# Causal attention in a decoder layer: who adds up the diagonal tiles, inverts the denominators and writes the upper output half

## What is computed

```python
x = _layernorm(x + _L0_attn_ref(x, Wqkv, Wout, bout))          # causal, 16 heads of 32
x = _layernorm(x + _L0_xattn_ref(x, ctx, ctx, mask, ...))      # cross attention
x = _layernorm(x + _L0_ffn_ref(x, w1, b1, w2, b2, ...))        # 8 experts, top 2

# _L0_attn_ref
qkv = x @ Wqkv.T
dots = where(causal_mask, -inf, einsum('bhid,bhjd->bhij', q, k) * dh**-0.5)
out = einsum('bhij,bhjd->bhid', softmax(dots), v)
return out @ Wout.T + bout
```

## Time and profile before

| | |
|---|---|
| median of 3 runs | 2791.89 us (2785.82 to 2792.28) |
| profiled execution | 2788.14 us, its span 2786.3 us |
| TensorE busy | 2563.3 us (92%) |
| VectorE busy | 1913.3 us (69%) |
| ScalarE busy | 1102.4 us (40%) |
| GpSimd busy | 782.0 us (28%) |
| self-attention within the span | about 290 to 1520 us |

### The profile page before, as it was taken

How to read it: one execution, slowest core, us unless ns; L and a number is a source line. 1 busy time by engine, 2 the same in 40 slices (tenths; PEclk the granted TensorE clock), 3 DMA queues, 4 the chain that set the end, 5 groups by cost and what they waited for, 6 DMA issues and landing times. The chain is left out here.

```text
span 2786.3 us, 44691 instructions
## 1 busy us (share of the span) xinstructions
PE 2563.3 (92%) x15124; PEld 1064.3 (38%) x15124; DVE 1913.3 (69%) x3125; ACT 1102.4 (40%) x2002; POOL 782.0 (28%) x276
## 2 busy tenths in 40 slices
PE   8999699998999899999998679999999999999998
PEld 3444223232232233332322335454544544454543
DVE  5442787877778677778882557776867676767764
ACT  4231155555555455555555223231323323232320
POOL 0000254553636344445455211111201011111100
PEclk9999799999999999999999889999999999999999
DMA  7953500302020302012001210101010101001000
GB/s 245 306 193 140 122 9 6 73 6 70 9 69 9 69 6 55 23 34 74 5 12 56 86 43 1 58 1 59 1 43 16 43 16 43 16 1 58 1 16 16
DMA packets 115902, 146.74 MB, mean 53 GB/s; under 512 B 9086, under 2 KB 87678, under 8 KB 114653
## 3 DMA queue, kind: packets, MB, share of 16 engines
q1 hardware_dynamic: 115677, 143.77, 16.9%
HBM read 91.57 MB, written 51.91 MB: 51 GB/s over the span
## 5 line engine op out<-in xcount | busy, mean ns | idle before, releaser
L715 ACT ACTIVATE probs<-st_ps 128x512 f32<-128x512 f32 (+3 forms) x1280 | 628.2, 533 | 590.5 <-PE st_ps L821 294.6
L746 DVE TENSOR_REDUCE seg_max<-s_ps 128x1 f32<-128x512 f32 (+3 forms) x1280 | 699.8, 599 | 230.3 <-PE s_ps L804 136.9
L804 PE MATMUL s_ps<-k_pair,q_pair 96*128 96x512 f16 (+3 forms) x1280 | 438.7, 364 | 70.0 <-DVE seg_max L746 56.4
L821 PE MATMUL st_ps<-q_pair,k_pair 98*128 98x512 f16 (+3 forms) x1280 | 434.6, 360 | 26.6 <-issue 19.5
L623 POOL TENSOR_TENSOR total<-total,probs 128x2048 f32<-128x2048 f32 x88 | 398.2, 4525 | 62.1 <-ACT probs L715 59.6
L841 PE MATMUL o_ps<-probs,v_sb 128*32 128x512 f32 (+3 forms) x2560 | 321.4, 572 | 0.7 <-issue 0.7
L1381 PE MATMUL fps<-x2T,w_p_hi 128*128 128x512 f16 x1024 | 317.2, 379 | 0.0
L1381 PE MATMUL fps<-w_p_hi,hT 128*128 128x512 f16 x1024 | 306.0, 381 | 0.0
L821 PEld LDWEIGHTS st_ps<-q_pair,k_pair 98*128 98x128 f16 x1280 | 117.5, 98 | 374.4 <-ACT probs L715 287.4
L804 PEld LDWEIGHTS s_ps<-k_pair,q_pair 96*128 96x128 f16 x1280 | 125.6, 99 | 276.9 <-DVE seg_max L746 191.3
L1343 DVE SCALAR_TENSOR_TENSOR x<-fps,gates_un,x 128x512 f32<-128x512 f32 x256 | 184.0, 746 | 36.0 <-PE fps L1381 33.4
(11 more groups left out here) (162 smaller groups left out, 3553.7 us busy)
## 6 DMA issues: line engine op xcount, KB each, us to landing
k_pair<-k_parts SPq DMA_DIRECT2D x96, 128.0 KB, 5.0
q_pair<-q_parts SPq DMA_DIRECT2D x96, 128.0 KB, 5.6
x_raw<-xT_in SPq DMA_DIRECT2D x8, 1024.0 KB, 6.5
q_parts<-qk_out SPq DMA_DIRECT2D x32, 256.0 KB, 3.6
k_parts<-qk_out SPq DMA_DIRECT2D x32, 256.0 KB, 4.0
piece_raw<-w_in SPq DMA_DIRECT2D x8, 1024.0 KB, 8.7
v_rows<-v_out SPq DMA_DIRECT2D x32, 256.0 KB, 2.1
w_parts<-piece_cut SPq DMA_DIRECT2D x8, 1024.0 KB, 5.6
```

Of the source, the lines that this page charges most:

```text
L715: nc.scalar.activation(probs[:, k % NP, h, off:], st_ps[:, p % (2 * NVU) % RING, off:], ACT.Exp, scale=SCALE).then_inc(exp_done.sem, 1)
L746: nc.vector.reduce_max(seg_max[:, h, j, s:s + 1], s_ps[:, slot, 0:width], AX.X).then_inc(s_read.sem, 1)
L804: last = nc.tensor.matmul(s_ps[:, slot, 0:width], q_pair[a][0:NR, h, q0:q0 + P], k_pair[a][0:NR, h, s * CH:s * CH + width], start=True, st ...
L821: last = nc.tensor.matmul(st_ps[:, slot, off:], k_pair[a][:, h, kt * P:(kt + 1) * P], q_pair[a][:, h, c * CH + off:(c + 1) * CH], start=Tr ...
```

## The change

- GpSimd also adds up all diagonal tiles, each over the columns that count. In chunk 0 the first addition starts at column 128, and a copy brings the rest. TensorE makes no sums for diagonal tiles any more; the matmuls over `total` become a step of their own, `totals`, with lag 8, in every chunk. `o_ready` goes (the values of the last tile count in `pv_done`), `den_ready` comes.
- ScalarE takes `den` with lag 9. One row of each head's 32 equal rows is moved to `inv_small`, 128 partitions x 16 columns (lag 10), VectorE inverts that (lag 16), SyncE stores it to a DRAM tensor `inv_rows` (17), and four broadcasting loads spread it over `inv` (21). GpSimd multiplies with lag 25.
- ScalarE instead of VectorE writes the upper half (lag 27), GpSimd the rest (28), the store has lag 29, and the tail of the plan is 30 steps instead of 21.
- `o_raw` and `den` get two buffers.

```diff
@@ -422,17 +422,20 @@
     NKU, NVU, NAUX = len(KU), len(VU), len(AUX)
-    POOLED = [[n for n, (k, kt) in enumerate(KU) if k == c and kt < c * TT and kt % 3 != 2]
+    POOLED = [[n for n, (k, kt) in enumerate(KU) if k == c and (kt >= c * TT or kt % 3 != 2)]
               for c in range(CPB)]
     ADDS = [n for tiles in POOLED for n in tiles[1:]]
     NP = 5
     RING = 3
-    PIECES = 4
     VALUES, SUMS = 4, 6
-    TAKEN = VALUES + 1, SUMS + 1
-    RECIPS = [SUMS + 3 + 2 * n for n in range(PIECES)]
-    SCALED = RECIPS[-1] + 1
+    TOTALS = 8
+    TAKEN = VALUES + 1, TOTALS + 1
+    DEN_MOVED = TAKEN[1] + 1
+    INVERTED = DEN_MOVED + 6
+    INV_STORED = INVERTED + 1
+    INV_LOADED = INV_STORED + 4
+    SCALED = INV_LOADED + 4
     STORED = SCALED + 4
     TAIL = STORED + 1
     READY = 6
...
@@ -447,8 +450,7 @@
         steps = [0.06 + 0.6 * (CH - off(c, kt)) / CH for c, kt, _ in VU]
         busy = [0.0] * NVU
         for t in LAST_TILE:
-            for lag in RECIPS:
-                busy[(t * HG + HG - 1 + lag) % NVU] += 0.85
+            busy[(t * HG + HG - 1 + INVERTED) % NVU] += 0.2
         cost = []
         for what, c, unit in AUX:
             if what == "rows":
...
@@ -549,8 +551,10 @@
-        o_raw = sb("o_raw", [P, CH], F32)
-        den = sb("den", [P, CH], F32)
+        o_raw = sb("o_raw", [P, 2, CH], F32)
+        den = sb("den", [P, 2, CH], F32)
+        inv_small = sb("inv_small", [P, 2, CH // DH], F32)
+        inv = sb("inv", [P, 2, CH], F32)
...
@@ -613,20 +619,26 @@
                     c, n = KU[k % NKU][0], adds_upto(k) - 1
                     starts = k % NKU == POOLED[c][1]
                     pool.wait_ge(exp_done.sem, exp_done.at(i, HG * k + HG - 1))
+                    off = max(KU[k % NKU][1] - c * TT, 0) * P
                     if starts:
-                        pool.wait_ge(pv_done.sem, pv_done.at(i, k // NKU * NKU + LAST_TILE[c - 1]))
+                        pool.wait_ge(den_ready.sem, den_ready.at(i, k // NKU * CPB + c - 1))
                         other = probs[:, (k // NKU * NKU + POOLED[c][0]) % NP]
                     else:
                         pool.wait_ge(added.sem, added.at(i, n - 1))
                         other = total[:]
-                    nc.gpsimd.tensor_tensor(total[:], other, probs[:, k % NP], ALU.add).then_inc(added.sem, 1)
+                    last = nc.gpsimd.tensor_tensor(total[:, :, off:], other[:, :, off:], probs[:, k % NP, :, off:],
+                                                   ALU.add)
+                    if starts and off:
+                        last = nc.gpsimd.tensor_copy(total[:, :, 0:off], other[:, :, 0:off])
+                    last.then_inc(added.sem, 1)
                 c = chunk_at(s, SCALED, first, end)
                 if c is not None:
-                    pool.wait_ge(recips.sem, recips.at(i, c * PIECES + PIECES - 1))
+                    pool.wait_ge(inv_loaded, 16 * HG * (2 * CPB * i + c + 1))
                     pool.wait_ge(split_done.sem, split_done.at(i, c - 1))
-                    nc.gpsimd.tensor_tensor(o_sb[:], o_raw[:], den[:], ALU.mult).then_inc(scaled.sem, 1)
+                    nc.gpsimd.tensor_tensor(o_sb[:], o_raw[:, c % 2], inv[:, c % 2],
+                                            ALU.mult).then_inc(scaled.sem, 1)
                 c = chunk_at(s, SCALED + 3, first, end)
                 if c is not None:
                     pool.wait_ge(o_hi_done.sem, o_hi_done.at(i, c))
...
@@ -674,6 +686,21 @@
                     sp.wait_ge(pv_done.sem, pv_done.at(i, k))
                     for c in range(CPB):
                         load(2 * i + k // NKU + 2, k // NKU % 2, c)
+                c = chunk_at(s, DEN_MOVED, first, end)
+                if c is not None:
+                    sp.wait_ge(den_taken.sem, den_taken.at(i, c))
+                    sp.dma_start(inv_small[:, c % 2], den[0:P:DH, c % 2]).then_inc(den_moved, 16)
+                c = chunk_at(s, INV_STORED, first, end)
+                if c is not None:
+                    sp.wait_ge(recips.sem, recips.at(i, c))
+                    sp.dma_start(inv_rows[c % 2].rearrange("h (a b) -> (h a) b", b=CH // DH),
+                                 inv_small[:, c % 2]).then_inc(inv_stored, 16)
+                c = chunk_at(s, INV_LOADED, first, end)
+                if c is not None:
+                    sp.wait_ge(inv_stored, 16 * (2 * CPB * i + c + 1))
+                    for h in range(HG):
+                        sp.dma_start(inv[h * DH:(h + 1) * DH, c % 2], inv_rows[c % 2, h].partition_broadcast(
+                            DH)).then_inc(inv_loaded, 16)
                 c = chunk_at(s, STORED, first, end)
                 if c is not None:
                     sp.wait_ge(split_done.sem, split_done.at(i, c))
...
@@ -716,19 +744,24 @@
                                          scale=SCALE).then_inc(exp_done.sem, 1)
                 c = chunk_at(s, TAKEN[0], first, end)
                 if c is not None:
-                    act.wait_ge(o_ready.sem, o_ready.at(i, c))
-                    act.wait_ge(scaled.sem, scaled.at(i, c - 1))
-                    nc.scalar.activation(o_raw[:], o_ps[:], ACT.Copy).then_inc(o_taken.sem, 1)
+                    act.wait_ge(pv_done.sem, pv_done.at(i, c // CPB * NKU + LAST_TILE[c % CPB]))
+                    act.wait_ge(scaled.sem, scaled.at(i, c - 2))
+                    nc.scalar.activation(o_raw[:, c % 2], o_ps[:], ACT.Copy).then_inc(o_taken.sem, 1)
                 c = chunk_at(s, TAKEN[1], first, end)
                 if c is not None:
-                    act.wait_ge(pv_done.sem, pv_done.at(i, c // CPB * NKU + LAST_TILE[c % CPB]))
-                    nc.scalar.activation(den[:], den_ps[:], ACT.Copy, scale=1.0 / XS).then_inc(den_taken.sem, 1)
+                    act.wait_ge(den_ready.sem, den_ready.at(i, c))
+                    nc.scalar.activation(den[:, c % 2], den_ps[:], ACT.Copy, scale=1.0 / XS).then_inc(den_taken.sem, 1)
+                c = chunk_at(s, SCALED + 2, first, end)
+                if c is not None:
+                    act.wait_ge(scaled.sem, scaled.at(i, c))
+                    act.wait_ge(o_stored[c % 2], stored_at(CPB * i + c // 2))
+                    nc.scalar.activation(o_out[:, c % 2, 0], o_sb[:], ACT.Copy).then_inc(o_hi_done.sem, 1)
             laps(act, step)
         @block.vector
         def _(dve):
-            for count in (s_read, max_ready, steps, recips, o_hi_done):
+            for count in (s_read, max_ready, steps, recips):
                 count.lead(dve)
             def aux(i, n):
...
@@ -758,18 +791,10 @@
             def step(i, s, first, end):
                 for n in aux_at(s, first, end):
                     aux(i, n)
-                for n, lag in enumerate(RECIPS):
-                    c = chunk_at(s, lag, first, end)
-                    if c is not None:
-                        if n == 0:
-                            dve.wait_ge(den_taken.sem, den_taken.at(i, c))
-                        piece = den[:, n * CH // PIECES:(n + 1) * CH // PIECES]
-                        nc.vector.reciprocal(piece, piece).then_inc(recips.sem, 1)
-                c = chunk_at(s, SCALED + 2, first, end)
+                c = chunk_at(s, INVERTED, first, end)
                 if c is not None:
-                    dve.wait_ge(scaled.sem, scaled.at(i, c))
-                    dve.wait_ge(o_stored[c % 2], stored_at(CPB * i + c // 2))
-                    nc.vector.tensor_copy(o_out[:, c % 2, 0], o_sb[:]).then_inc(o_hi_done.sem, 1)
+                    dve.wait_ge(den_moved, 16 * (2 * CPB * i + c + 1))
+                    nc.vector.reciprocal(inv_small[:, c % 2], inv_small[:, c % 2]).then_inc(recips.sem, 1)
             for n in range(AHEAD):
                 aux(0, n)
...
@@ -842,27 +867,28 @@
                                             start=(kt == 0), stop=final)
                 if k % NKU in POOLED[c]:
                     last.then_inc(pv_done.sem, 1)
-                elif final:
-                    last.then_inc(o_ready.sem, 1)
             def sums(i, k):
                 c, kt = KU[k % NKU]
-                off, pooled = max(kt - c * TT, 0) * P, POOLED[c]
-                final = k % NKU == LAST_TILE[c]
-                if k % NKU in pooled:
+                if k % NKU in POOLED[c]:
                     return
-                opens = all(n in pooled for n, (x, _) in enumerate(KU) if x == c and n < k % NKU)
+                opens = all(n in POOLED[c] for n, (x, _) in enumerate(KU) if x == c and n < k % NKU)
                 if opens:
                     pe.wait_ge(den_taken.sem, den_taken.at(i, k // NKU * CPB + c - 1))
                 for h, out in enumerate(heads):
-                    last = nc.tensor.matmul(den_ps[out, off:], ones[:], probs[:, k % NP, h, off:], start=opens,
-                                            stop=final and not pooled)
-                if final and pooled:
-                    pe.wait_ge(added.sem, added.at(i, adds_upto(k) - 1))
```

(16 more changed lines are left out.)

14 lines of the change are left out of this document (9 added, 5 removed).

## The result

The changed kernel takes 2861.27 us, median of four runs (2857.15 to 2866.8); the kernel before, beside it, 2790.48 us (2785.82 to 2792.28). The ratio is 1.0258, with an interval of 1.0235 to 1.0280. So the change makes the kernel 2.6% slower. The forecast was slower too, and 2861 lies inside the range, but the size is far off: 20 us were forecast, 71 came.

The account below looks back on a forecast made before the run. TensorE was taken as the bound. From 2788.1 us, 61 gained in eight groups, 75 lost to denominators waiting behind loads and 6.7 at the stage's end gave 2808.8, taken as 2808; range 2735 to 2870.

Parts of the forecast that it names:

- VectorE's wait behind the loads: At the end of 6 of 8 groups, chunk 3's denominator transfer queues behind SyncE's loads: VectorE stands 18 us, TensorE 15.5.
- 3.7 for the clock: After TensorE's stall behind the loads: further loss at lower clock, 3.7 us for each of six sets of loads.
- 3.5 absorbed: After the stall behind loads, slow steps absorb chunk 3's ScalarE wait: 3.5 us taken off each, 21 in all.
- Rival 1: SyncE's queue: small transfer held only behind the loads' issue, not their data; TensorE stands 9 us; total 2769; chance 0.16.
- ScalarE's two long waits: Upper half's wait for GpSimd's multiplication: 4.5 us for chunk 3, 6 for chunk 0; TensorE stands 2.9 and 4.8.
- Rival 2: Behind `max_parts`, VectorE's subtraction waits out a second, back-to-back GpSimd addition: 4.52 us once a group; total 2844; chance 0.17.
- Rival 3: Queues absorb it: ScalarE's waits vanish in TensorE's lead, a group takes 131 us; total 2741; chance 0.17.
- rival 4: Whole kernel: gain and loss cancel, the work merely changes its owner; total 2788; chance 0.12.
- the last diagonal addition ends before TensorE asks for it: GpSimd's queue, followed at the tile pace: its diagonal sums are ready before TensorE needs them, two tiles later.
- a stretch at half clock: TensorE behind a stall: part of the following time runs at 1.2 instead of 2.4 GHz, costing about 1.7 us each.
- The chain behind it: End of the stage, from `den` through small transfers and reciprocal to the last store: issued 6.7 us later, uncovered.
- a gain of 12.0 us a group: VectorE's casts removed: 6.9 us of TensorE's idle time and 5.1 us at half clock taken as gone.

Follow-up runs that it names:

- g4: Changed kernel with ScalarE's upper half, GpSimd's subtraction and the store six steps later, loads left in place: 2817.56 us, 1.0102 against the kernel before.
- e1: Changed kernel with SyncE's loads moved away from the groups' ends, 78 and 126 steps after: 2755.8 us, 0.9880 against the kernel before.
- f1: e1 with ScalarE's upper half, GpSimd's subtraction and the store six steps later: 2708.77 us, 0.9717 against the kernel before.
- g1: f1 with ScalarE instead of VectorE scaling the row maxima into `max_parts`: 2663.29 us, 0.9549 against the kernel before.
- g2: g1 with the last chunk's diagonal sums on TensorE in the last group only: 2651.87 us, 0.9500 against the kernel before.
- e2: Control: kernel before the change with the loads moved to the same two places as in e1: 2782.36 us, 0.9976 against the kernel before.
- f4: Kernel before with only GpSimd's diagonal additions and two buffers for denominators and raw outputs: 2900.25 us, 1.0404 against the kernel before.
- f2: e1 with the sums over diagonal tiles back on TensorE: 2761.77 us, 0.9908 against the kernel before.
- e4: Changed kernel with the `max_parts` scaling written as an operation with two SBUF inputs: 2863.92 us, 1.0266 against the kernel before.
- f3: e1 with the upper half written by VectorE instead of ScalarE, at the same step: 2750.43 us, 0.9864 against the kernel before.

## Why the prediction was right or wrong

**Where the miss lies.** In the profiled executions 20.7 us were forecast and 69.0 measured. Of the 48.3 us between them 21.8 lie in the six groups between the cuts, 20.2 in the two groups outside them with the end of the stage, 6.2 in the second half.

**Right: the mechanism, and the price of the wait partly by luck.** VectorE's wait behind the loads was forecast at 18 us, TensorE's at 15.5: 17.19 and 16.54. One set of loads was to cost 15.5 + 3.7 for the clock - 3.5 absorbed, 15.7 us: 15.2. But the last two terms are both wrong and cancel. In a group with loads (611.43 to 772.06) TensorE still waits 8.2 us for ScalarE, against 7.9 in the one without, so nothing is absorbed, and g4 says the same. Its busy time there is 129.7 us against 129.2, so the clock adds 0.5 and not 3.7. What the six groups of before already held of it (19.6) is also right: 901.3 us are 6 x 147.0 and 19.3. And e1 shows by experiment what the trace could only suggest. Rival 1 (a shorter wait) fell: the transfer was held by both the issue order and its own issue of 6.24 us.

**Right: what moved.** GpSimd's 114.7 us a group are 115.15. TensorE waits 61.7 us for ScalarE, which is 7.7 a group, as forecast, and again two errors cancel. ScalarE's two long waits were forecast at 4.5 and 6 us, of which the score banks were to keep 2.8 from TensorE; they are shorter, and TensorE stands 3.71 and 4.20 us behind them, so that only 0.5 is kept. The four waits of ScalarE in the group without loads are 3.82, 4.61, 0.82 and 0.43 us. These are the rows of the first two:

```profile
1448.07 0.63 ACT L758 ACTIVATE o_out<-o_sb 128x512 f16<-128x512 f32 x1 [3.82 <-POOL o_sb L640]
1467.27 0.63 ACT L758 ACTIVATE o_out<-o_sb 128x512 f16<-128x512 f32 x1 [4.61 <-POOL o_sb L640]
```

TensorE waits 28.0 us for `max_parts`, 3.5 a group against 3.8 forecast. Rival 2 fell for the changed kernel: the subtraction behind takes 176 ns on average over 30, with GpSimd busy for 80% of a group. Its mechanism is real all the same and was a matter of 0.1 us: f1's rows show it at 4.42 us once a group, which is what the rival had said. Rival 3 (the queues absorb it) fell by the 61.7 us above, rival 4 (nothing) by the result.

**Wrong: the ordinary group, 143.5 us and not 139.4.** That is 4.1 us in each of the eight, 33 in all; the 21.8 and the 20.2 us above both hold their share of it. Two terms of the sum failed. The first is the sentence "the last diagonal addition ends before TensorE asks for it". It doesn't:

```profile
1373.72 1.93 PE L890 MATMUL den_ps<-total,ones 128*32 128x512 f32 x8 [2.38 <-POOL total L630]
```

That happens once a group, 17.4 us in the eight groups, 2.2 a group. I had followed the queue at a pace of 2.75 us for a diagonal tile, but its additions take 4.5 and 3.4 us for the first two, and by my reading the queue was not empty when they came. The prediction named this very wait as what would prove it wrong. The second is the clock. TensorE's busy time came out at 129.15 us where the terms gave 127.1 (138.1 - 11.0, less the 5.1 us for the casts, plus 3.4 and 1.7). I had charged a stretch at half clock that loses 1.7 us for each of three stalls. Before, that is right: behind the stalls of 1.78, 2.27 and 2.59 us the granted clock falls to 0.50 (1.2 instead of 2.4 GHz) and is back at 1.00 within 6 us, and the stretches lose 1.7 us each (2 us times what the granted clock of each 2 us is short of 1.00). In the ordinary group of the changed kernel there are four, behind stalls of 2.38, 2.93, 3.71 and 4.20 us, and they lose 1.6, 1.7, 3.1 and 2.1 us: 8.6 and not 5.1. The stall for the total is one of them. TensorE's busy time shows only 2.0 of the 3.5 us; where the rest went I can't say. g1 shows the same from the other side: with stalls of at most 1.8 us a mean clock of 0.99 and 124.5 us busy. The two make 2.2 + 2.0 of the 4.1 us.

**Wrong: the two groups outside the cuts and the end of the stage, 20.2 us.** Forecast for the two groups outside the cuts and the end was -15.2 + 6.7 = -8.5 us; measured is -5.5 + 17.2 = +11.7. 8.2 of it are again the 4.1 us a group. The larger part is in these rows, on GpSimd, TensorE, GpSimd and SyncE in turn:

```profile
1536.62 30.67 POOL L630 TENSOR_TENSOR total<-total,probs 128x2048 f32<-128x2048 f32 x8
```
```profile
1567.34 1.93 PE L890 MATMUL den_ps<-total,ones 128*32 128x512 f32 x8 [8.94 <-POOL total L630]
```
```profile
1576.88 1.26 POOL L640 TENSOR_TENSOR o_sb<-o_raw,inv 128x512 f32<-128x512 f32 x1 [9.59 <-DMA inv<-inv_rows]
```
```profile
1580.06 0.40 SPq L709 DMA_DIRECT2D o_parts<-o_out  x1
```

Eight additions run without a gap up to 1567.3, while the last exponential ended at 1557.9. In the last chunks there are no maxima to find, so tiles come faster than GpSimd can add them. The last store is 22.2 us behind the last exponential (before 9.1): 13 us more and not 6.7. The step that failed is that I priced the chain behind `den` but took `den` itself as no later. ScalarE starts to copy `den` 11.4 us after the last exponential, where it was 2.1: 9.4 us that stand nowhere in the sum. The chain behind it is 3.6 us longer and not 6.7, as the small transfers are quicker than I took them. (The sign that I gave, some 12 us to the last store, did not even fit my own sum, which makes it 9.1 + 6.7 = 15.8.) g2 confirms the step: 11.4 us come back where TensorE sums these four tiles itself. The last group up to its last exponential was also 4.2 us longer than before (153.3 against 149.1), with 11.6 us of waits for exponentials and 3.7 for a total in it; I did not separate these further.

**Open: 6 us in the second half.** Its program is the same, and it takes 1272.0 us in the changed kernel and in e1 against 1265.8 before and 1266.3 in e2, but 1267.2 in g1. About half is lost early in it. It need not come from the change: over all fourteen profiled kernels, with the same second half, it takes 1264.7 (f4) to 1272.2 us (f2), and 1268.0 in e4, which differs from the changed kernel by one short instruction. No run isolates the cause.

**Rests on a wrong picture though no number fell with it:** I had counted the removed casts as a gain of 12.0 us a group that comes with ScalarE's copy. f3 says that the copy's engine is worth nothing at this place (0.9864 against 0.9880): there a cast on VectorE takes 0.42 us. In f4 it takes 3.6. What makes a cast dear is an addition that GpSimd starts ahead of it, so it was the new place behind the multiplication that took the hold away, and not ScalarE. What the copy costs at that place is the wait for the multiplication, and that goes when it stands later (f1).
